# Leaving out 15 unused TensorE products in the last full attention slot of a fused two-layer kernel

## The reference, cut to what matters

```
        latent_kv = x @ w_kv_down
        kv = latent_kv @ w_kv_up
        k, v = (kv[..., :HD], kv[..., HD:])
...
        q = (x @ w_q).reshape(Bx, Tx, N_HEAD, HEAD_SIZE)
        scale = HEAD_SIZE ** (-0.5)
        att = jnp.einsum('bqhd,bkhd->bhqk', q, k) * scale
        causal = jnp.tril(jnp.ones((Tx, Tx), dtype=bool))
        att = jnp.where(causal, att, -jnp.inf)
        att = jax.nn.softmax(att, axis=-1)
        y = jnp.einsum('bhqk,bkhd->bqhd', att, v)
        y = y.reshape(Bx, Tx, HD)
        return y @ w_out
...
        y = jnp.einsum('bnh,boh->bno', x, W) + b[:, None, :]
...
        h = jax.nn.gelu(_bitlinear(x, w1), approximate=False)
        return _bitlinear(h, w2)
```

## Time and profile before

| | before |
|---|---|
| median of 3 executions | 1346.37 us (1346.17 to 1348.09) |
| the profiled execution's own time | 1348.85 us |
| its span in the profile | 1345.9 us |
| mean granted TensorE clock | 0.996 |
| busy over the span | PE 94%, DVE 83%, POOL 82%, ACT 76% |
| L636 over the whole kernel | 90 products, each with a weight load |

### The profile page before, as it was taken

One profiled execution on the slowest core, in us unless ns is written; L12 is line 12 of the kernel. 1 busy time (PEld: TensorE's weight loads), 2 busy tenths in 40 slices (PEclk: granted clock), 3 DMA queues, 4 the chain that ended last, 5 costly groups with the idle time before them and its releaser, 6 DMA issues.

```text
span 1345.9 us, 20424 instructions
## 1 busy us (share of the span) xinstructions
PE 1270.2 (94%) x5650; PEld 722.9 (54%) x5651; DVE 1114.8 (83%) x1625; ACT 1019.0 (76%) x2553; POOL 1099.1 (82%) x645
## 2 busy tenths in 40 slices
PE   8899999999999999999999999989989999999997
PEld 4344344344344344344344356689985666766676
DVE  3999999999999999999999989755646566665655
ACT  4878888888988988988888888433336787787785
POOL 5799999999999999999999999445427766756562
PEclk9999999999999999999999999999989999999999
DMA  5664274165164255255345372423311000000000
GB/s 189 244 268 176 95 290 206 74 267 207 72 280 206 97 243 206 106 246 206 131 208 207 138 257 87 134 60 98 102 44 28 11 20 18 19 17 17 9 6 12
DMA packets 49356, 178.50 MB, mean 133 GB/s; under 512 B 15688, under 2 KB 33292, under 8 KB 40700
## 3 DMA queue, kind: packets, MB, share of 16 engines
q1 hardware_dynamic: 46988, 172.74, 33.5%
q0 software_dynamic: 2272, 4.66, 1.5%
HBM read 169.71 MB, written 16.52 MB: 138 GB/s over the span
## 4 chain that ended last, share of the span: by engine, by line
PE 36%; DVE 26%; issue 18%; ACT 11%; POOL 5%; DMA 1%; SPq 1%; DVEq 1%; POOLq 0%; another core or an unknown queue 0%; ACTq 0%
DVE h L1530 18%; DVE h L1511 5%; ACT banks L1492 5%; PE banks L459 4%; PE banks L816 4%; PE banks L889 4%; PE banks L863 4%; POOL h L1536 4%; PE banks L793 2%; PE banks L756 2%; PE banks L773 2%; PE banks L468 2%; PE banks L1565 2%; PE banks L904 2%; ACT L1363 2%
## 5 line engine op out<-in xcount | busy, mean ns | idle before, releaser
L1536 POOL TENSOR_TENSOR h<-h,Cb 128x1024 f32<-128x1024 f32 (+2 forms) x166 | 583.5, 3571 | 9.0 <-DVE h L1530 8.6
L1530 DVE TENSOR_TENSOR_SCAN h<-banks,h 128x1024 f32<-128x1024 f32 x256 | 569.0, 2272 | 5.9 <-ACT banks L1492 4.6
L1492 ACT ACTIVATE banks<-dt,A_cur 128x255 f32<-128x255 f32 x1024 | 424.0, 462 | 75.2 <-DVE h L1530 72.4
L1565 PE MATMUL banks<-h,ident 128*128 128x512 f32 x1024 | 471.5, 600 | 5.9 <-DVE yz L1574 1.7
L1565 PEld LDWEIGHTS banks<-h,ident 128*128 128x128 f32 x1024 | 186.6, 190 | 242.1 <-issue 197.2
L1511 DVE TENSOR_TENSOR h<-Bb,banks 128x1024 f32<-128x1024 f32 (+2 forms) x101 | 199.8, 1997 | 0.6
L1517 POOL TENSOR_TENSOR h<-Bb,u 128x1024 f32<-128x1024 f32 (+1 forms) x50 | 185.5, 3713 | 1.9 <-DVE xs L1433 1.8
L855 POOL TENSOR_SCALAR h<-h 128x128 f32<-128x128 f32 (+1 forms) x128 | 97.4, 777 | 50.4 <-DVE h L839 50.3
L855 POOL TENSOR_SCALAR Cb<-Cb,h 128x128 f32<-128x128 f32 x124 | 94.7, 780 | 37.8 <-DVE h L839 37.7
L1319 PE MATMUL banks<-xn,wF 128*128 128x512 f32 x256 | 114.7, 599 | 2.2 <-ACT xn L1311 2.2
L1319 PEld LDWEIGHTS banks<-xn,wF 128*128 128x128 f32 x256 | 48.0, 190 | 64.6 <-issue 61.5
(11 more groups left out here) (379 smaller groups left out, 2020.9 us busy)
## 6 DMA issues: line engine op xcount, KB each, us to landing
Cb<-scrX SPq DMA_DIRECT2D x32, 2048.0 KB, 8.9
Bb<-scrX SPq DMA_DIRECT2D x31, 2048.0 KB, 11.8
by_expert<-in_x SPq DMA_DIRECT2D x15, 576.0 KB
h<-in_L_ffn_w SPq DMA_DIRECT2D x2, 2048.0 KB, 8.8
by_expert<-Cb SPq DMA_DIRECT2D x39, 64.0 KB
h<-in_conv_w SPq DMA_DIRECT2D x4, 512.0 KB, 4.5
Bb<-scrX SPq DMA_DIRECT2D x2, 1024.0 KB, 5.8
scr<-Cb SPq DMA_DIRECT2D x3, 640.0 KB, 3.0
```

The lines of the kernel that those rows point to most:

```text
L1492: m = e.activation(ps_dA[c % 2][:, g, half, 1:S], dts[q][:, half, i * S + 1:(i + 1) * S], ACT.Exp, scale=A_cur[q][:, s:s + 1])
L1530: e.tensor_tensor_scan(chunk(i, c), ps_dA_flat[c % 2], chunk(i, c), 0.0, ALU.mult, ALU.add).then_inc(sem("scan"), 1)
L1536: e.tensor_tensor(h[i][:, rows(cs), :, :], h[i][:, rows(cs), :, :], both(Cb[i], cs), ALU.mult).then_inc(sem("hC"), len(cs))
L1565: m = e.matmul(bank(5), ident[:], h_flat[i][:, s * HALVES * S:(s + 1) * HALVES * S], start=(s == 0), stop=(s == NS - 1))
```

## The change

It takes `warm:4`, `warm:9` and `warm:2` out of slot 7 of TensorE's list. The 2 products at the end of that slot and all of those in `ENDING` stay.

```
-           fqturn fu:0 turn:8 score:7 turn:9 fu:1 values:3 turn:10 values:4 turn:11 warm:4 turn:12 warm:9 turn:13
-           values:5 warm:2 fq2turn turn:14 turn:15 values:6 fd values:7"""},
+           fqturn fu:0 turn:8 score:7 turn:9 fu:1 values:3 turn:10 values:4 turn:11 turn:12 turn:13
+           values:5 fq2turn turn:14 turn:15 values:6 fd values:7"""},
```

## The result

| | before | changed |
|---|---|---|
| median of 20 executions | 1347.35 us (1344.95 to 1349.58) | 1345.57 us (1342.86 to 1349.29) |
| profiled execution: own time | 1348.85 us | 1344.60 us |
| its span | 1345.9 us | 1342.8 us |
| its mean granted clock | 0.996 | 0.996 |

The ratio is 0.9986, with a 95% interval of 0.9980 to 0.9992: 1.8 us less in the medians, where 1.9 were forecast. The change is clear of its interval, but its size is within the 0.2% that the forecast called no change. The range of 1343.8 to 1347.2 us holds 1345.57. The absolute forecast of 1344.5 is a microsecond low because it stood on a median of three, 1346.37, where twenty give 1347.35.

What follows compares the result with a forecast made beforehand. The prediction took TensorE, without a wait from 1320.56 us to the last value product, to bound the kernel. Of 3.54 us removed about 1.6 return as waiting, so 1346.37 - 1.9 = 1344.5 us, range 1343.8 to 1347.2.

Steps and rivals of the forecast that it cites:

- The sum: Slot 7: 3.54 us of products go, about 1.6 come back as TensorE's waiting, 1.9 us stay won.
- Turn of head 12: Slot 7: starts at about 1320.6 us instead of 1321.45, after DVE's copy of head 10; 0.15 us of waiting.
- Turn of head 13: Slot 7: waits 1.2 us for ACT's copy of head 11, starts at 1322.15 us instead of 1323.79; 1.64 won.
- Turns of heads 14 and 15: Slot 7: bounded by DVE's norm; head 14 starts at 1323.8 us, 15 at 1324.35 instead of 1326.34; 2.0 won.
- The 2 products: Ahead of fq2turn, 0.64 us on the chain; without them it starts at 1323.3 us instead of 1325.56, 2.26 won.
- Behind it all moves along: From values:6 into the ending: all comes earlier, values:7 by 1.9 us, with the ending's rows the same lengths.
- clock rival: Clock halves at about 1322 us: shortly (1346.2 or 1347.9, chance 0.11) or to the end (1356.5 at most, 0.08).
- A short fall: Clock halves at about 1322 us for 3.41 or 6.83 us, costing 1.7 or 3.4; chance 0.11.
- Rival 3: Slot 7: ACT's copy of head 11 or DVE's norms come later, saving only 0 to 1.2 us; chance 0.08.
- Rival 4: Slot 7: all 3.54 us are won, giving 1342.8 us; chance 0.05, shared with a lucky measurement.
- The starting point: Whole kernel: median of the executions shown, 1346.37 us, from which 1.9 was taken to forecast 1344.5.

## Why the prediction was right, and where not

- **The sum.** 3.54 us out, 1.9 us won was forecast; 1.71 in the profile and 1.8 in the medians. The interval of the ratio is 1.1 to 2.7 us, so the medians cannot tell 1.7 from 1.9, and that they come as close as 0.1 is luck in part; the profile is what tests the terms. The mechanism was right: TensorE, late for everything in the stretch, becomes early for three of its turns. Shown by the runs that take one group at a time. Of the 3.54 us 1.83 came back, where about 1.6 were forecast: 1.14 us of idle time ahead of the three turns (0.13, 0.95 and 0.06), 0.57 in their open starts, 0.10 in fq2turn and 0.02 in the turn of head 14.
- **Turn of head 12.** Forecast 0.15 us of waiting; it cost 0.32, a wait of 0.13 and an open start of 0.19. Undersized, without effect on the end, as the time lies ahead of head 13's wait.
- **Turn of head 13.** Forecast 2.94 us behind `values:4` (1322.15 - 1319.21), measured 2.95, released by ACT's copy of head 11. The wait itself is 0.95 us and not the 1.2 forecast, mostly because the turn of head 12 ahead of it took 0.17 us more than I gave it; the date did not depend on that. For the turn itself I gave 0.35 us where the chain has 0.52: the open start.
- **Turns of heads 14 and 15.** The forecast named two dates that meet at head 15, DVE's norm and ACT's turned:13, and called the norm the bound. In the changed kernel ACT is last, by 0.06 us; that the norm is the floor right under it is shown by the run with the copy behind prob:14. Head 15 was to start 5.14 us behind `values:4` and starts at 5.23, `values:6` 5.54 and at 5.75. These 0.2 us are what 1.9 was too high by, and the step that was off is the price of a wait: two turns on this path (heads 13 and 15) with an open start of 0.19 us each, of which I had counted next to nothing for head 13 and a part for head 15.
- **The 2 products.** The step "With the 2 products gone it starts at 1323.3 instead of 1325.56: here 2.26 us are won" let them count for 0.64 on the way. They are worth 0.28, since fq2turn was not alone in holding the turns behind it: ACT's turned:13, which starts from `values:5`, held head 15.
- **Behind it all moves along.** Ending 15.51 before, 15.50 after: right.
- **Rivals.** The clock did not fall in the stretch in any profile, although TensorE had 1.87 us of work in the 3.68 us ahead of head 13's turn, so in the profiles neither clock rival has its place there. A short fall does occur, in the ending, also with the ending left as it is, and costs 1.35 us in that one execution. Whether the change makes falls more frequent is open, by the clocks of the executions above; it did not move the median. Rival 3 (the copy of head 11 or the norms come later) did not happen: the copy starts 2.33 us behind `values:4` before and after, the norms 3.99 and 4.01. Rival 4 (all 3.54 us won) lies outside the interval. The rule of the Trainium skill that short idle times between groups of matmuls can lower the clock (TensorE: Matmul & The Clock Gate, "A second HAM failure mode: psum-queue depth-cycling") is compatible with the ending, where no gap above 0.61 us stood ahead of a fall; but the same gaps kept full clock in the other profiles, and in the stretch it is not seen.
- **The starting point.** The median of three was 1 us under that of twenty; the difference was forecast, the absolute value only as well as its base.

## What to carry to other kernels

Work that fills time on an engine is worth what lies between it and the next date that another engine sets, so price each piece by the chain behind it, and leave those that fall into a wait alone: 4 of the 15 products here cost nothing, though they would have been worth 0.58 us had the 9 behind them stayed. A wait on TensorE ahead of these fp32 turns cost its length and 0.19 us more, for the overlap that is lost. When the effect is a thousandth, measure between two instructions of one profile, on either side of the edit; the start of one and the same instruction, behind identical code, differed by twice the effect.

## What was not expected of the hardware

- The granted clock fell in one of nine profiles with the same, unchanged ending, behind 3.5 us in which TensorE did the same work, with no gap over 0.61 us, as in profiles that kept full clock; it cost 1.35 us. In the slot ahead, 2.52 us in 5.0 kept full clock. Why the one and not the other is open.
- A gap in TensorE's timeline can be a record that is missing: 1.37 us here, of which the piece that reads the missing product's output gives the true picture.
- Moving a copy ahead of the first exponential moved the table load (1.28 us) behind that copy's wait, and cost 1.5 us in the stretch.
